# GpSimd adds the halves of each head's squares of q, VectorE sums what is left behind the rotation of k

## The reference, cut to what matters

```python
def l2norm(t):
    return t / jnp.maximum(jnp.linalg.norm(t, axis=-1, keepdims=True), 1e-12)
...
q, k, v = (sh(q), sh(k), sh(v))      # 16 heads of 64 values
q = l2norm(q) * qs
k = l2norm(k) * ksc
q = q * cos * scale + rotate_half(q) * sin * scale
k = k * cos * inv + rotate_half(k) * sin * inv
out = local_attention(q, k, v)       # windows of 32, own and previous
```

## Time and profile before

| | us |
|---|---|
| median of 3 runs | 3413.21 (3407.72 to 3415.92) |
| profiled execution, whole | 3412.6 |
| its span, first to last instruction | 3410.8 |

### The profile page before, as it was taken

One profiled execution on the slowest core, in us unless ns is written; L12 is line 12 of the kernel. 1 busy time (PEld: TensorE's weight loads), 2 busy tenths in 40 slices (PEclk: granted clock), 3 DMA queues, 4 the chain that ended last, 5 costly groups with the idle time before them and its releaser, 6 DMA issues. The chain is left out here.

```text
span 3410.8 us, 100964 instructions
## 1 busy us (share of the span) xinstructions
PE 3286.0 (96%) x42193; PEld 2145.6 (63%) x42193; DVE 2796.2 (82%) x4519; ACT 2299.8 (67%) x4541; POOL 2259.8 (66%) x1364
## 2 busy tenths in 40 slices
PE   8999699999999999999999999999999999999996
PEld 5555366666666666666666666666666666666663
DVE  2333698998988888989898889898999888988893
ACT  2222367777776777777777777777777777776774
POOL 0000377877777777777777777777777777777772
PEclk9999899999999999999999999999999999999998
DMA  2000001000001000001000010000010000000000
GB/s 73 1 1 1 4 11 36 11 11 11 8 17 36 10 10 11 11 16 34 11 11 11 8 42 11 11 9 11 11 42 8 11 11 11 12 13 17 15 8 13
DMA packets 62281, 52.50 MB, mean 15 GB/s; under 512 B 11526, under 2 KB 59396, under 8 KB 61828
## 3 DMA queue, kind: packets, MB, share of 16 engines
q1 hardware_dynamic: 61828, 46.05, 5.3%
HBM read 43.93 MB, written 2.10 MB: 13 GB/s over the span
## 5 line engine op out<-in xcount | busy, mean ns | idle before, releaser
L448 POOL TENSOR_TENSOR cosp<-cosp,rr 128x1024 f32<-128x1024 f32 x384 | 723.1, 1904 | 591.8 <-DVE rr L992 591.7
L458 POOL TENSOR_TENSOR cosp<-cosp,sinp 128x1024 f32<-128x1024 f32 x384 | 903.3, 2373 | 21.2 <-DVE sinp L971 21.2
L568 PE MATMUL ps<-w_qk,xs 128*128 128x512 f32 x1536 | 761.1, 618 | 24.1 <-ACT sq L776 19.7
L672 PEld LDWEIGHTS ps<-px,w_vo 128*128 128x128 f32 x6144 | 700.9, 192 | 54.1 <-ACT px L824 48.5
L672 PE MATMUL ps<-px,w_vo 128*128 128x128 f32 x6144 | 725.0, 276 | 3.1 <-ACT px L824 1.7
L776 ACT ACTIVATE sq<-ps 128x1024 f32<-128x1024 f32 x384 | 393.1, 1024 | 462.5 <-DVE sinp L971 462.5
L968 DVE TENSOR_TENSOR cosp<-ps,tab 128x1024 f32<-128x1024 f32 x384 | 469.3, 1222 | 110.7 <-PE ps L568 109.4
L568 PEld LDWEIGHTS ps<-w_qk,xs 128*128 128x128 f32 x1536 | 262.5, 190 | 387.2 <-issue 380.7
L977 DVE TENSOR_REDUCE ss<-sq 128x16 f32<-128x1024 f32 x384 | 455.4, 1186 | 57.5 <-ACT sq L776 57.2
L971 DVE TENSOR_TENSOR sinp<-ps,tab 128x1024 f32<-128x1024 f32 x384 | 466.3, 1214 | 0.0
L575 PEld LDWEIGHTS ps<-ident,cosp 128*128 128x128 f32 x3072 | 354.0, 142 | 117.0 <-DVE xb L1038 74.3
(11 more groups left out here) (107 smaller groups left out, 4437.3 us busy)
## 6 DMA issues: line engine op xcount, KB each, us to landing
tab<-in_tab SPq DMA_DIRECT2D x96, 128.0 KB, 2.1
qks<-in_scales SPq DMA_DIRECT2D x96, 128.0 KB, 3.4
w_qk<-in_L_ffn_Wqkv SPq DMA_DIRECT2D x12, 512.0 KB, 6.7
w_v<-in_wv_t SPq DMA_DIRECT2D x6, 512.0 KB, 8.2
w_o<-in_L_ffn_Wo SPq DMA_DIRECT2D x6, 512.0 KB, 9.3
x<-in_L_attn_x SPq DMA_DIRECT2D x16, 128.0 KB, 5.7
out<-w_v SPq DMA_DIRECT2D x16, 128.0 KB, 2.4
w<-in_L_ffn_W SPq DMA_DIRECT2D x6, 341.0 KB
```

What stands on the lines that cost most here:

```text
L448: eng.tensor_tensor(v, v, rr[:, B % 2, HEADS * i:HEADS * i + HEADS].unsqueeze(2).to_broadcast([P, HEADS, DH]), ALU.mult).then_inc(rot_read ...
L458: eng.tensor_tensor(cosp[:, A % 2, i, :], cosp[:, A % 2, i, :], sinp[:, i, :], ALU.add).then_inc(rot_added, 1)
L568: t = eng.matmul(ps[:, u, :], xs[:, n % ROUND, :], w_qk[:, n // TILES % 2, i, 512 * u:512 * u + 512], start=True, stop=True)
L672: t = eng.matmul(Y, w_vo[:, E // TILES % 2, i // HP, i % HP, :], px[:, i, :], start=i == 0, stop=i == HEADS - 1)
```

## The change

The sum of the squares of q is made in two parts. GpSimd adds, in place, the upper 32 squares of each head to the lower 32 (128 x 512 elements out), behind the two scalings of tile B and ahead of `pn`. VectorE then reduces the 32 remaining values of each head instead of 64, and does so behind the two instructions that rotate k rather than ahead of `xb`. It waits there for the new semaphore `halves_done`. The sum for k is as before.

```diff
@@ GpSimd
+            def add_halves(n, i):
+                eng.wait_ge(sq_done, 2 * n + i + 1)
+                v = sq[:, i, :].rearrange("p (h u f) -> p h u f", u=2, f=32)
+                eng.tensor_tensor(v[:, :, 0, :], v[:, :, 0, :], v[:, :, 1, :], ALU.add).then_inc(halves_done, 1)
...
+                if tile(A):
+                    add_halves(A, 0)
                 if tile(C):
                     eng.wait_ge(recip_done, C + 1)
@@ VectorE
             def square_sum(n, i):
-                eng.wait_ge(sq_done, 2 * n + i + 1)
                 if i == 0:
+                    eng.wait_ge(halves_done, n + 1)
                     after(eng, norm_step, normed(n))
-                eng.tensor_reduce(ss[:, HEADS * i:HEADS * i + HEADS], sq[:, i, :].rearrange("p (h d) -> p h d", d=DH),
-                                  AX_X, ALU.add).then_inc(ssq_done, 1)
+                    parts = sq[:, 0, :].rearrange("p (h u f) -> p h u f", u=2, f=32)[:, :, 0, :]
+                else:
+                    eng.wait_ge(sq_done, 2 * n + 2)
+                    parts = sq[:, 1, :].rearrange("p (h d) -> p h d", d=DH)
+                eng.tensor_reduce(ss[:, HEADS * i:HEADS * i + HEADS], parts, AX_X, ALU.add).then_inc(ssq_done, 1)
...
-                if tile(A):
-                    square_sum(A, 0)
                 if tile(E):
                     eng.wait_ge(y_done, E + 1)
...
                 if tile(A):
                     rope(A, 1)
+                    square_sum(A, 0)
```

More of the change, by code:

```diff
@@ L240, in build @@
         sq_done = sem("sq_done")
+        halves_done = sem("halves_done")
         ssq_done = sem("ssq_done")
```

## The result

The changed kernel takes 3453.4 us (median of 4 runs, 3452.03 to 3455.67), the kernel before 3414.57 us beside it: a ratio of 1.0108 with a 95% interval of 1.0092 to 1.0124. Forecast were 3447 us, +1.0%, and a range of 3420 to 3474. Between the two medians lie 38.8 us. The profiled execution took 3455.67 us, the slowest of the four, with a span of 3453.9, against 3410.8 before: 43.1 us more of span.

The account below looks back on a forecast made before the run. VectorE's ring through ACT and PE was taken to bind in phases 3, 0 and early steps, PE elsewhere. 19.2 + 9.9 + 1.6 + 3.6 = 34.3 us on 3412.6 gave 3447 us, +1.0%, range 3420 to 3474.

Parts of the forecast that it names:

- Sum of q out of its old place: VectorE ahead of `xb`: 1.18 us leave, but the 0.51 us wait for k's projection grows to about 1.6; booked 0.
- Half sum in the ring: VectorE between rotation of k and `pT`: 0.60 us, paid in phase 3 of 32 turns (19.2 us), 0 in phases 0 to 2.
- the ring: Chain from rotation of k through VectorE, ACT's square and PE's projection to the next rotation; said to bind in phases 3 and 0.
- cover by delays of PE: 16 of 48 turns where PE was late for its own reasons, so VectorE's delay was taken as covered; they pay 0.1 each.
- Signs in phase 2: VectorE's waits before the sum of k (0.45 us) and the `px` copy should shrink as the half sum uses them.
- Variance and ACT's copies: Phase 3: variance 1.25 us later delays ACT's guess and `px` copies, PE 0.75; free up to 1.25 us of GpSimd operation.
- Root steps held by `hh`: Phase 0: GpSimd's later `hh` holds VectorE's first root step, 0.31 us in 32 turns (9.9), 0.1 in 16 (1.6).
- The early steps: Six steps before the first feed-forward piece, without idle time to cover the half sum: 0.60 us each, 3.6 together.
- A: Rival: GpSimd's halves take longer than `hh` because of gapped operands; 3473 at 1.6 us, 3490 to 3510 at 2.37; chance 0.14.
- D: Rival: VectorE's halved reduction takes as long as the whole, 1.11 us; 29 us more, 3476; chance 0.05.
- B: Rival: PE sets the pace in phases 3 and 0 too and hides the cost, within 0.2%, 3418; chance 0.12.
- C: Rival: the turn of k starts when `xb` allows, so earlier `xb` returns 0.41 us in 192 steps; 3368, faster; chance 0.07.

Follow-up runs that it names:

- few_q: Kernel before, with the sum of q taken over 2 of the 64 squares of each head, in the old place: 3410.7 us, ratio 0.9994.
- whole_in_3_0: Changed kernel, but steps of phases 3 and 0 do as before (whole sum of q in the old place, no halves on GpSimd): 3414.9 us, ratio 1.0014.
- whole_in_3: Changed kernel, but steps of phase 3 do as before (whole sum of q in the old place, no halves on GpSimd): 3426.4 us, ratio 1.0044.
- move_only: Kernel before, with VectorE's whole sum of q moved behind the rotation of k and nothing new on GpSimd: 3484.8 us, ratio 1.0204.
- halves_only: Kernel before, VectorE unchanged, plus GpSimd adding the halves of q's squares into a spare bf16 tile nobody reads: 3434.5 us, ratio 1.0064.
- whole_in_0: Changed kernel, but steps of phase 0 do as before (whole sum of q in the old place, no halves on GpSimd): 3439.0 us, ratio 1.0066.
- halves_at_end: As halves_only, but GpSimd adds the halves last in each step, behind the variance and the hh products: 3425.4 us, ratio 1.0028.
- memset_at_end: As halves_at_end, but GpSimd writes zeros three times over the spare tile instead and reads nothing: 3414.2 us, ratio 0.9992.
- few_k: Kernel before, with the sum of k taken over 2 of the 64 squares of each head, in its place: 3382.9 us, ratio 0.9923.

## Why the prediction was right, and where its terms were off

Sign, size and mechanism held: 3453 for 3447, 38.8 us between the medians for 34.3. That the total came so near is in part luck, since several terms were off and one cause, the clock, was in none of them. By its steps (some of its row numbers are off: the wait of 0.52 us and the sum of 1.18 us stand in the earlier trace rows, and the idle times of phase 1, told there as not shown, in the earlier trace rows):

**Sum of q out of its old place, worth 0.** Right. The wait ahead of the rotation of k went to 1.64 us (1.6 foretold), and `few_q` took the sum away for no gain.

**Half sum in the ring.** 0.60 us from start to start foretold, 0.59 measured; 0 in phases 1 and 2, shown by `whole_in_3_0`; in full in phase 3, shown by `whole_in_3`. That the place costs, and not GpSimd, is shown by `move_only`. The term of 19.2 us is the one that was mis-sized most: it came to 27 in the profiled execution. Of the 46 steps into phase 0, 34 grew by 0.58 to 0.77 us (21.6 us together), where 32 of 48 were foretold; 5 grew by 0.34 or less (-0.3 us together), so the cover by delays of PE that I gave to 16 turns is there in fewer. The other 7 had the lower clock in one of the two executions or in both, and make up the remaining 6.0 us, by between -1.95 and 3.6 each. I had no term for these.

**Signs in phase 2.** The wait ahead of the sum of k went as foretold, from 0.45 us to none. The wait ahead of the `px` copy hardly shrank, from 0.91 to 0.87 us in the median: the first idle time covered nearly all of the half sum.

**Variance and ACT's copies.** Foretold as free up to 1.25 us of GpSimd's operation (it took 1.26). Right to within 0.1 us in turns without fusion; in the 20 with fusion PE's own path grows by 0.7, which is 0.1 more than the ring's 0.6. Since the two run side by side and the later one counts, this adds only some 2 us to the change; alone it is most of what `halves_only` loses (0.7 x 20 = 14 of some 22 us). The error was to take PE's room in phase 0 from one turn that had no fusion in it.

**Root steps held by `hh`.** 9.9 + 1.6 foretold, 8.4 measured into phase 1. The mechanism was right. Of the 46 steps into phase 1 in the changed kernel, 29 have a held root step and grew by 0.29 us in the median; the other 17 grew by 0.00. `whole_in_0`, which takes the half sum out of phase 0 as well, can't tell the two apart by itself; these 17 can, since they have the half sum too, and so can `halves_at_end`, which brings the 0.3 back with another GpSimd operation, beside `memset_at_end`, which doesn't (15.15 and 14.81). The counting was loose. The prediction gave 0.1 us to turns with fusion, every second one, but put the 0.1 into the sum for the 16 turns that it took as covered by delays of PE. Measured into phase 1 were 14.99 us behind a step with fusion and 15.14 behind one without, against 14.81 in both before.

**The early steps.** 3.6 foretold, 6.3 measured. Four of them grew by 0.6 to 0.8; the rest of the difference is the step of 18.6 us, in which the granted clock was at 0.50, together with steps that were shorter. `whole_in_0` has the same long step; what the idle time of PE ahead of it comes from isn't shown.

**The rivals.** A (GpSimd slower than `hh`) and D (the halved reduction as slow as the whole) fall with the two durations, 1.26 and 0.68 us, though A's chain through ACT's copies does bind in turns with fusion. A's upper figure was also added up wrong: 1.1 + 1.1 us in 32 turns and half of that in 16 is 88 us, 3535 and not 3490 to 3510. B (hidden by PE) falls with the growth into phase 0 (its 97% for PE in a steady turn is 99% in the turn of the earlier trace rows), and C (the residual as the bound) with `few_q` and with the result: `xb` came 1.1 us sooner and the step into phases 2 and 3 didn't change.

Apart from `few_k`, which leaves out most of k's sum, none of the kernels is faster than the kernel before. `few_k` shows that some 28 us lie in that part of the sum; the runs show no way to take it out of the ring.

## What to carry to other kernels

Before moving work off a busy engine, ask on which side of its wait the work stands: in front of a wait it is free already, and taking nearly all of it away gave nothing that could be measured (ratio 0.9994), while half of it put behind the wait made up most of a loss of 1%. Follow the ring through all engines until it meets its own start, and look for idle time in each phase of the pipeline, in the rarer ones too (here the turns with weight fusion), because here two neighbouring chains were within 0.1 us of each other and only the later one was visible. An operation on an engine with room to spare still delayed what was queued behind it, and what that met on other engines. And a single profiled execution carries accidents of its own, here about 9 us with the granted clock: compare the medians of steps of one kind, not only the sums.

## What the runs showed of the hardware

A VectorE instruction with two operands from SBUF was held until a GpSimd instruction that reads SBUF had ended: 0.18 us became up to 0.64 us, in 30 steps of the changed kernel and 72 of `halves_at_end`, and each of them ended within 0.07 us of the GpSimd instruction. Beside GpSimd instructions that only write (the zeros, 1.70 us of them) it was not held: in `memset_at_end` 294 of the five small root steps started while zeros were being written, and the longest of them took 0.20 us. That is what the Trainium skill states ("SBUF — State Buffer", Who interferes with whom), and these traces agree with both halves of it. The held time shows as a longer VectorE instruction and not as idle time ahead of it, so a view of waits doesn't have it.

I had not expected that gaps in the operands (runs of 32 of 64 values) cost GpSimd nothing: 1266 ns for the halves, 1271 ns for `hh` of the same size without gaps.

PE's matmuls took close to twice as long while the granted clock was at 0.50: 3.80 us for 16 matmuls that take 2.00 at full clock.
